# A gated recurrence on TensorE: 448-column f16 matmuls between its dependent matmuls, and its bias rows as two-row f16 matmuls

## The chip, the core and the metric

One core of one Trainium2 chip runs the whole program in one launch. The metric is the device time of one execution in microseconds (us). TensorE (PE; its weight loads are PEld) does the matmuls and writes PSUM, VectorE (DVE) and ScalarE (ACT) read PSUM and do the elementwise work, GpSimd (POOL) does memsets, copies and indirect DMAs, SyncE (SP) issues most transfers. Each has its own instruction stream; they meet at semaphores.

## What is computed

Four layers are applied to x of shape 8 x 512 x 256. Only the first has the part that is changed, a GRU over 512 time steps:

```python
def step(h, inp):                       # h: 8 x 256, one x_t of 8 x 256 a step
    x_t, prop = inp
    comb = jnp.concatenate([x_t, h], axis=-1)
    z = jax.nn.sigmoid(comb @ Wz + bz)
    r = jax.nn.sigmoid(comb @ Wr + br)
    comb2 = jnp.concatenate([x_t, r * h], axis=-1)
    h_cand = jnp.tanh(comb2 @ Wh + bh)
    h_new = (1.0 - z) * h + z * h_cand
    h_next = jnp.where(prop, jnp.tanh(h_new @ Wp + bp), h_new)
    return (h_next, h_new)
```

`prop` is true on every fourth step. What follows (a mixture-of-experts layer, a second one, a linear state-space layer with an LSTM-like layer, and a top-k layer) is not touched.

## The kernel before

Everything of the recurrence is held transposed: feature on the partition, batch of 8 on the free axis, two halves (k, m) of 128 features. The f32 hidden state is scaled by 256 and split into two f16 parts, `hpart[:, 0]` (high) and `hpart[:, 1]` (the rest); the recurrent weights are split likewise in `wpart`. A product with a gate is then 8 matmuls on part 0 and, once part 1 is there, 4 more (`recur`, L1418), each with 128x128 f16 weights of its own and 8 moving columns.

512 steps are made in 32 turns of 16. Each turn has four PSUM banks: r, z, candidate (c), and p, the bank of the propagated state. Of the p bank columns 0 to 63 are used. While one turn is stepped through, the input's share and the biases of the next turn are put into the other four banks by a generator, `projections`: for each of r, z, c and each half m, one f32 bias matmul with one row (`gbias` times `ones`, L1398) and two f32 matmuls of 128 columns with the input (`wx` times XT, L1402); then two f32 bias matmuls of 32 columns for p (L1406). These 20 items of a turn are taken one by one: one behind each step's c product, and one behind each of the four p products. PE's order within a step is: r (24 instructions with z), then c, then an item, and on every fourth step p, then an item. An f32 matmul shows as two instructions in the trace.

ACT reads the r, z, c (and p) banks with a tanh each; DVE makes `rhpart` from r and h (L905, L906, L908) and `hpart` from z, the candidate and h (L919 to L924). PE's loop runs over pairs of turns, so it branches back 15 times.

Ahead of the recurrence x is transposed on PE and copied by DVE to XT, ACT and DVE split the weights (L880), and DVE scales the biases (L883), which the first projections wait for.

Of the kernel before, what the change touches and what calls it, by code (L numbers as in the profile page):

```python
# [19 lines left out]
ALU = mybir.AluOpType  # L20
# [14 lines left out]
GSCALE = HSCALE * WSCALE  # L35
E = 8
# [22 lines left out]
def build_program(nc, t, out):  # L59
    ctx = ExitStack()  # L60
    with ctx:
        def sb(name, shape, dt=F32):
            return ctx.enter_context(nc.sbuf_tensor(name, shape, dt))
# [23 lines left out]
        gbias = sb("gbias", [1, 4, D])  # L87
# [17 lines left out]
        zeros = WA[:, 0:ZW]  # L105
        strict = sb("strict", [P, P])
# [114 lines left out]
        gru_b_loaded = sem("gru_b_loaded")  # L221
        wsplit, wsplit_high = sem("wsplit"), sem("wsplit_high")
        condT_psum = sem("condT_psum")
        condT_ready = sem("condT_ready")
# [5 lines left out]
        keep_ready, keep_h_ready, upd_ready = sem("keep_ready"), sem("keep_h_ready"), sem("upd_ready")  # L230
# [91 lines left out]
        def _(sp):  # L322
# [13 lines left out]
            for g, n in enumerate(("br", "bz", "bh", "bp")):  # L336
                sp.dma_start(gbias[0:1, g], t["L0_cond_" + n].rearrange("(a m) -> a m", a=1)).then_inc(gru_b_loaded, 16)
# [38 lines left out]
            sp.wait_ge(prefer_ready, E + 8)  # L376
# [84 lines left out]
            sp.wait_ge(prefer_ready, E + 9)  # L461
# [24 lines left out]
        def _(pool):  # L486
            nc.gpsimd.memset(ident[:], 0.0).then_inc(ident_zero, 1)
# [6 lines left out]
            nc.gpsimd.memset(ones16[:], 1.0).then_inc(prefer_ready, 1)  # L494
            nc.gpsimd.memset(strict[:], 1.0).then_inc(prefer_ready, 1)
            nc.gpsimd.memset(zeros, 0.0).then_inc(prefer_ready, 1)
            pool.wait_ge(prefer_ready, E + 6)
# [371 lines left out]
        def _(dve):  # L869
            for k in range(KD):  # L870
# [11 lines left out]
            dve.wait_ge(gru_b_loaded, 5 * 16)  # L882
            nc.vector.tensor_scalar(gbias[:], gbias[:], GSCALE, None, ALU.mult).then_inc(wsplit, 1)  # L883

            dve.wait_ge(condT_psum, 1)
            nc.vector.tensor_copy(condT[:].rearrange("p k b -> p (k b)"), banks[6][:, 0:KD * B]).then_inc(condT_ready, 1)
# [12 lines left out]
            with dve.Fori(0, TURNS) as it:  # L899
                for s in range(STEPS):  # L900
                    n = it * STEPS + s
                    h = entry_s[:] if s % CHUNK == 0 else hist[:, s - 1]

                    dve.wait_ge(r_ready, n + 1)
                    nc.vector.scalar_tensor_tensor(rhpart[:, 0], gate_r[:], 1.0, h, ALU.add, ALU.mult).then_inc(rh_part, 1)  # L905
                    nc.vector.scalar_tensor_tensor(rfull[:], gate_r[:], 1.0, h, ALU.add, ALU.mult).then_inc(rh_full, 1)  # L906
                    dve.wait_ge(rh_full, n + 1)
                    nc.vector.tensor_tensor(rhpart[:, 1], rfull[:], rhpart[:, 0], ALU.subtract).then_inc(rh_part, 1)  # L908

                    dve.wait_ge(z_ready, n + 1)  # L910
                    nc.vector.tensor_scalar(keep[:], gate_z[:], -0.5, 0.5, ALU.mult, ALU.add).then_inc(keep_ready, 1)
                    dve.wait_ge(keep_ready, n + 1)
                    nc.vector.tensor_tensor(keep_h[:], keep[:], h, ALU.mult).then_inc(keep_h_ready, 1)
                    if s % (STEPS // 2) == 0:

                        dve.wait_ge(hist_copied, it * 2 + 1 + s // (STEPS // 2))

                    dve.wait_ge(c_ready, n + 1)
                    nc.vector.scalar_tensor_tensor(upd[:], gate_z[:], 1.0, cand[:], ALU.add, ALU.mult).then_inc(upd_ready, 1)  # L919
                    dve.wait_ge(upd_ready, n + 1)  # L920
                    nc.vector.scalar_tensor_tensor(hpart[:, 0], upd[:], 0.5 * HSCALE, keep_h[:], ALU.mult, ALU.add).then_inc(h_part, 1)  # L921
                    nc.vector.scalar_tensor_tensor(hist[:, s], upd[:], 0.5 * HSCALE, keep_h[:], ALU.mult, ALU.add).then_inc(h_full, 1)  # L922
                    dve.wait_ge(h_full, n + 1)
                    nc.vector.tensor_tensor(hpart[:, 1], hist[:, s], hpart[:, 0], ALU.subtract).then_inc(h_part, 1)  # L924
                    if (s + 1) % CHUNK == 0:
                        split_entry(it * NP + (s // CHUNK + 2))

            link = Link(dve, vc)
# [61 lines left out]
            dve.wait_ge(prefer_ready, E + 8)  # L990
# [377 lines left out]
        def _(pe):  # L1368

            pe.wait_ge(const_ready, 2)  # L1370
# [8 lines left out]
            pe.wait_ge(gru_b_loaded, 5 * 16)  # L1379
# [6 lines left out]
            pe.wait_ge(gru_b_loaded, 5 * 16)  # L1386
# [6 lines left out]
            def projections(it, r_bank, z_bank, c_bank, p_bank):  # L1393

                for g, bank in enumerate((r_bank, z_bank, c_bank)):
                    for m in range(KD):
                        o = bank[:, m * W:(m + 1) * W]
                        nc.tensor.matmul(o, gbias[0:1, g, m * P:(m + 1) * P], ones[0:1, 0:W], start=m == 0, stop=False,  # L1398
                                         skip_group_check=True)
                        yield  # L1400
                        for k in range(KD):
                            nc.tensor.matmul(o, wx[:, g, k, m * P:(m + 1) * P], xview[:, k, bass.ds(it * STEPS, STEPS)],  # L1402
                                             start=False, stop=False, skip_group_check=True)
                            yield
                for m in range(KD):
                    nc.tensor.matmul(p_bank[:, m * NP * B:(m + 1) * NP * B], gbias[0:1, 3, m * P:(m + 1) * P],  # L1406
                                     ones[0:1, 0:NP * B], start=m == 0, stop=False, skip_group_check=True)
                    yield
# [479 lines left out]
```

## Time and profile before

| | us |
|---|---|
| median of 3 runs | 3479.25 (3477.07 to 3480.55) |
| span of the profiled execution, first to last instruction | 3475.2 |
| median less span, what lies around it | 4.05 |
| transposes, splits and first projections | 0 to 42.6 |
| recurrence | 42.6 to 1411 |
| everything after it | 1411 to 3475.2 |

The profiled execution has no time of its own listed beside its span, so the median of the runs stands for it. PE is busy for 2975.7 us (86%), DVE for 1343.1 (39%), ACT for 850.8 (24%), POOL for 431.1 (12%). Busy time of PE is from the start of a matmul to its modelled end, so overlapping matmuls fill it even where the engine moves few columns. The granted TensorE clock has two levels in this trace, 0.5 (1.2 GHz) and 1.0 (2.4 GHz).

### The profile page before, as it was taken

Reading aid. Unit: us, or ns where it says so; the run is one execution under the profiler, and the core shown is the slowest. Engines: PE = TensorE matmul, PEld = TensorE weight load, DVE = VectorE, ACT = ScalarE, POOL = GpSimd, SP = SyncE. Lnnn points to the kernel's source line nnn. Section 1 sums busy time; section 2 is a strip of 40 time slices with the busy share of each in tenths; the row PEclk is TensorE's granted clock in tenths of the full one; section 3 lists DMA queues with packets and bytes.
Section 4 is the critical chain, followed back from the end, with each engine's and each line's share of the span. In section 5 each row is a group of like instructions: output and inputs, shape, how many; then the busy total and the mean of one; then the engine's idle time right before and its main releaser. Section 6 shows DMA issues by size and latency. Waiting matters only on the chain.

```text
span 3475.2 us, 75119 instructions
## 1 busy us (share of the span) xinstructions
PE 2975.7 (86%) x28154; PEld 2213.9 (64%) x28154; DVE 1343.1 (39%) x6282; ACT 850.8 (24%) x2694; POOL 431.1 (12%) x510
## 2 busy tenths in 40 slices
PE   7888888888888888529999995789965898999888
PEld 6777777777777777318888883345841343388367
DVE  4555555555555555301111002433333356511442
ACT  1222222222222222112223221123521112322332
POOL 0000000000000000240000003343143000000343
PEclk6555555555555555659999997989987999899989
DMA  5000000000000000036666663312434431000123
GB/s 189 2 2 2 2 2 2 2 2 2 2 2 2 2 2 2 32 126 191 190 190 191 193 197 93 95 60 91 127 100 138 91 73 24 0 0 0 35 80 106
DMA packets 182176, 230.13 MB, mean 66 GB/s; under 512 B 57492, under 2 KB 146168, under 8 KB 181432
## 3 DMA queue, kind: packets, MB, share of 16 engines
q1 hardware_dynamic: 159704, 162.01, 16.4%
q0 software_dynamic: 22240, 64.51, 5.6%
q8 instruction: 209, 3.42, 0.4%
q14 instruction: 23, 0.19, 0.0%
HBM read 166.31 MB, written 60.16 MB: 65 GB/s over the span
## 4 chain that ended last, share of the span: by engine, by line
issue 46%; PE 44%; DVE 3%; DMA 2%; another core or an unknown queue 1%; POOL 1%; ACT 1%; SPq 1%; ACTq 0%; DVEq 0%; POOLq 0%
PE bank L1556 8%; PE bank L1568 8%; PE bank L1754 5%; PE bank L1513 3%; PE bank L1502 3%; PE bank L1614 2%; PE bank L1682 2%; PE bank L1671 2%; PE bank L1855 2%; PE bank L1867 2%; PE bank L1623 1%; PE bank L1716 1%; PE bank L1543 1%; PE bank L1789 1%
## 5 line engine op out<-in xcount | busy, mean ns | idle before, releaser
L1418 PEld LDWEIGHTS bank<-hpart,WB 128*128 128x128 f16 x13824 | 464.5, 105 | 229.4 <-DVE hpart L921 162.8
L1418 PE MATMUL bank<-hpart,WB 128*128 128x8 f16 x13824 | 520.4, 170 | 71.2 <-issue 45.3
L1418 PE MATMUL bank<-rhpart,WB 128*128 128x8 f16 x6144 | 288.1, 171 | 85.3 <-DVE rhpart L905 85.3
L1418 PEld LDWEIGHTS bank<-rhpart,WB 128*128 128x128 f16 x6144 | 242.3, 106 | 131.1 <-DVE rhpart L905 128.6
L1556 PE MATMUL bank<-WA,WB 128*128 128x256 f32 x1248 | 309.2, 381 | 8.7 <-DMA WA<-in_L_ffn_b 8.7
L1568 PE MATMUL bank<-WB,hid 128*128 128x256 f32 x1248 | 313.8, 379 | 0.0
L1402 PE MATMUL bank<-XT,WB 128*128 (+1 forms) x792 | 305.1, 482 | 0.9
L1556 PEld LDWEIGHTS bank<-WA,WB 128*128 128x128 f32 x1248 | 238.1, 191 | 41.7 <-issue 9.1
L1568 PEld LDWEIGHTS bank<-WB,hid 128*128 128x128 f32 x1248 | 234.2, 190 | 30.3
L1013 DVE COPY WA<-bank 128x512 f32<-128x512 f32 x76 | 52.6, 692 | 514.6 <-PE bank L1543 514.6
L671 ACT ACTIVATE hid<-bank,b_up 128x256 f32<-128x256 f32 x312 | 148.0, 475 | 394.2 <-PE bank L1556 394.2
L596 ACT ACTIVATE gate_r<-bank 128x16 f32<-128x16 f32 x512 | 94.7, 185 | 598.0 <-PE bank L1418 598.0
L1402 PEld LDWEIGHTS bank<-XT,WB 128*128 128x128 f32 x792 | 198.6, 312 | 4.8 <-issue 1.3
L510 POOL TENSOR_TENSOR HT<-hist,unscale 128x128 f32 x64 | 29.5, 460 | 1374.2 <-DVE hist L922 1374.2
L600 ACT ACTIVATE cand<-bank 128x16 f32<-128x16 f32 x512 | 94.2, 184 | 279.2 <-PE bank L1418 279.2
L1398 PE MATMUL bank<-ones,gbias 1*128 1x128 f32 x396 | 156.5, 496 | 3.8 <-DVE gbias L883 3.8
L905 DVE SCALAR_TENSOR_TENSOR rhpart<-gate_r,hist 128x16 f16<-128x16 f32 x384 | 67.5, 176 | 223.0 <-ACT gate_r L596 223.0
L919 DVE SCALAR_TENSOR_TENSOR upd<-gate_z,cand 128x16 f32<-128x16 f32 x512 | 90.0, 176 | 149.7 <-ACT cand L600 149.7
L523 POOL DMA_INDIRECT tile_rows<-WA,slots x128 | 123.4, 964 | 158.3 <-ACT WA L708 77.2
L528 POOL DMA_DIRECT2D expert_rows<-WA x78 | 56.0, 718 | 696.5 <-DVE WA L1024 530.0
L543 POOL DMA_INDIRECT WA<-expert_rows,slots x128 | 121.7, 951 | 90.5 <-DVE WA L1035 46.8
L1614 PE MATMUL bank<-XT,WB 128*128 (+1 forms) x256 | 118.3, 611 | 7.7 <-DVE WB L1076 7.6
(305 smaller groups left out, 4010.6 us busy)
## 6 DMA issues: line engine op xcount, KB each, us to landing
WB<-in_L_ffn_w SPq DMA_DIRECT2D x78, 1024.0 KB, 7.8
WA<-tile_rows SPq DMA_DIRECT2D x86, 256.0 KB
expert_rows<-WA POOLq DMA_DIRECT2D x86, 256.0 KB, 2.7
GB<-gates SPq DMA_DIRECT2D x8, 2048.0 KB
tile_rows<-WA SPq DMA_DIRECT2D x4, 2496.0 KB, 17.6
WA<-in_L_ffn_b SPq DMA_DIRECT2D x40, 128.0 KB, 7.3
GB<-in_x SPq DMA_DIRECT2D x8, 512.0 KB, 7.1
out<-HT SPq DMA_DIRECT2D x16, 256.0 KB
```

What stands on the lines that cost most here:

```text
L523: nc.gpsimd.indirect_dma_start(xg, bass.IndirectOffsetOnAxis(ap=slots[:, c, b:b + 1], axis=0), hrow[:, q], None).then_inc(moved[q], 16)
L543: nc.gpsimd.indirect_dma_start(grow[:, q, c], None, yg, bass.IndirectOffsetOnAxis(ap=slots[:, c, b:b + 1], axis=0)).then_inc(moved[q], 16)
L671: nc.scalar.activation(hid0[:, f], banks[f % RING][:, 0:ET], ACT.Gelu, bias=b0_up[:, i, f:f + 1]).then_inc(S["hid_ready"], 1)
L1398: nc.tensor.matmul(o, gbias[0:1, g, m * P:(m + 1) * P], ones[0:1, 0:W], start=m == 0, stop=False, skip_group_check=True)
L1402: nc.tensor.matmul(o, wx[:, g, k, m * P:(m + 1) * P], xview[:, k, bass.ds(it * STEPS, STEPS)], start=False, stop=False, skip_group_check=True)
L1418: last = nc.tensor.matmul(bank[:, m * width + s * B:m * width + (s + 1) * B], wpart[:, g, w, k, m * P:(m + 1) * P], part[:, a, k * B:(k + ...
L1502: last = nc.tensor.matmul(banks[f % RING][:], up(f, k), src(k), start=k == 0, stop=k == KD - 1)
L1513: last = nc.tensor.matmul(banks[4 + m][:], down(h, m), hid[:, h % RING], start=h == 0 and not out_extra, stop=h == n - 1)
L1556: last = nc.tensor.matmul(banks[f % RING][:, 0:ET], w0_up[i][:, k, f * P:(f + 1) * P], xgT[:, i, k], start=k == 0, stop=k == KD - 1)
L1568: last = nc.tensor.matmul(banks[4 + m][:, 0:D], hid0[:, h, half_of(m)], w0_down[i][:, h], start=h == 0, stop=h == F0 - 1)
L1614: last = nc.tensor.matmul(banks[u % RING][:], (wsh1, wsh3)[u % 2][:, k, u // 2 * P:(u // 2 + 1) * P], XT[:, k, cols(j)], start=k == 0, sto ...
L1754: last = nc.tensor.matmul(banks[h * 3 + g][:, m * 256:(m + 1) * 256], uT[:, g + 4 * part, k, half_of(m)], src, start=not part and m == 0 a ...
```

## The change

Two things are done in the recurrence, and the start is rearranged for them.

1. `keep_clock` issues f16 matmuls of 448 columns with operands that are always there (`wpart`) into columns 64 to 511 of the next turn's p bank, which nothing reads. One stands between z and c in each step, two behind the item after c, one behind the item after p, and one more at either place where the item was a bias.
2. A bias item becomes one f16 matmul with two rows: the high and the low f16 part of the bias (`gbias_part`) times 256 (`bias_unit`). It has no f32 matmul any more.
3. Ahead of the first projections 24 matmuls of 512 columns on ones are issued (`BURST`). The bias loads are issued first of all DMAs, with a semaphore of their own for `condrow`; DVE splits the biases ahead of its copies of x; POOL makes the constants for it first. Two unused semaphores go.

```diff
+BURST = 24
+STREAM = 2
...
+            for g, n in enumerate(("br", "bz", "bh", "bp")):
+                sp.dma_start(gbias[:, g], t["L0_cond_" + n].rearrange("(a m) -> a m", a=1).partition_broadcast(2)).then_inc(gru_b_loaded, 16)
             for j in range(B // 2):
                 load_x(j)
-            sp.dma_start(condrow[:], t["cond_1024"]).then_inc(gru_b_loaded, 16)
+            sp.dma_start(condrow[:], t["cond_1024"]).then_inc(condrow_loaded, 16)
...
+            dve.wait_ge(gru_b_loaded, 4 * 16)
+            dve.wait_ge(row_made, 4)
+            link(nc.vector.tensor_scalar(gbias, gbias, HSCALE, None, ALU.mult))
+            link(nc.vector.tensor_copy(gbias_hi, gbias))
+            link(nc.vector.tensor_tensor(gbias_rest, gbias, gbias_hi, ALU.subtract))
+            link(nc.vector.tensor_scalar(gbias_rest, gbias_rest, part_row[:, 1:2], None, ALU.mult))
+            nc.vector.scalar_tensor_tensor(gbias_part, gbias_hi, part_row[:, 0:1], gbias_rest, ALU.mult, ALU.add
+                                           ).then_inc(wsplit, 1)
...
+            ones512 = ones16[:].rearrange("p (a c) -> p a c", a=1).to_broadcast([P, 512 // P, P])
+            for i in range(BURST):
+                nc.tensor.matmul(banks[7][:], ones16[:], ones512, start=i == 0, stop=i == BURST - 1)
             pe.wait_ge(gru_w_loaded, 7 * 16)
...
-                        nc.tensor.matmul(o, gbias[0:1, g, m * P:(m + 1) * P], ones[0:1, 0:W], start=m == 0, stop=False,
+                        nc.tensor.matmul(o, gbias_part[:, g, m * P:(m + 1) * P], bias_unit[:, 0:W], start=m == 0, stop=False,
                                          skip_group_check=True)
-                        yield
+                        yield True
...
+            spare = slice(KD * NP * B, 512)
+            stream = wpart[:, 3, 0].rearrange("p k m -> p (k m)")[:, spare]
+
+            def keep_clock(bank, count):
+
+                for _ in range(count):
+                    nc.tensor.matmul(bank[:, spare], wpart[:, 3, 0, 0, 0:P], stream, start=False, stop=True, skip_group_check=True)
...
                     recur(gates[1], 1, W, s, hpart, None).then_inc(z_psum, 1)
+                    keep_clock(next_gates[3], 1)
                     recur(gates[2], 2, W, s, rhpart, lambda a: pe.wait_ge(rh_part, n * 2 + a + 1)).then_inc(c_psum, 1)
-                    next(following, None)
+                    light = next(following, True)
+                    keep_clock(next_gates[3], STREAM + light)
                     if (s + 1) % CHUNK == 0:
                         recur(gates[3], 3, NP * B, s // CHUNK, hpart,
                               lambda a: pe.wait_ge(h_part, n * 2 + a + 1)).then_inc(p_psum, 1)
-                        next(following, None)
+                        light = next(following, True)
+                        keep_clock(next_gates[3], 1 + light)
```

PE's order in a step of the loop, before. L1418 are the products, L1402 an input item, L1398 a bias item; ISA and REGISTER_ALU are waits and counting:

```order
L1402 ISA
L1402 MATMUL bank<-XT,WB 128x128
L1418 MATMUL bank<-hpart,WB 128x8 x24
L1435 ISA
L1418 MATMUL bank<-rhpart,WB 128x8 x8
L1435 REGISTER_ALU
L1418 MATMUL bank<-rhpart,WB 128x8 x4
L1398 MATMUL bank<-ones,gbias 128x128
L1418 MATMUL bank<-hpart,WB 128x8 x12
L1402 MATMUL bank<-XT,WB 128x128
```

PE's order at the same place of the changed kernel. L1440 are the products, L1452 the new 448-column matmuls, L1424 an input item, L1420 a bias item:

```order
L1424 ISA
L1424 MATMUL bank<-XT,WB 128x128
L1452 MATMUL bank<-WB 128x448 x2
L1440 MATMUL bank<-hpart,WB 128x8 x24
L1452 MATMUL bank<-WB 128x448
L1466 ISA
L1440 MATMUL bank<-rhpart,WB 128x8 x8
L1466 REGISTER_ALU
L1440 MATMUL bank<-rhpart,WB 128x8 x4
L1420 MATMUL bank<-WA 128x128
L1452 MATMUL bank<-WB 128x448 x3
L1440 MATMUL bank<-hpart,WB 128x8 x12
```

The new matmuls stand between z's product and c's, and between the items and the next product on `hpart`; no product has changed its place among the others. A turn has 60 of them: 16 behind z, 32 and 6 behind the items after c, 4 and 2 behind the items after p.

PE's order ahead of the recurrence, before and then changed (transposes, then the first projections):

```order
L1377 MATMUL bank<-ident,GB 128x128 x64
L1381 MATMUL bank<-ident,condrow 128x8 x2
L1398 MATMUL bank<-ones,gbias 128x128
L1402 MATMUL bank<-XT,WB 128x128 x2
L1398 MATMUL bank<-ones,gbias 128x128
```

```order
L1397 MATMUL bank<-ident,GB 128x128 x64
L1401 MATMUL bank<-ident,condrow 128x8 x2
L1407 MATMUL bank<-ones 128x512 x24
L1420 MATMUL bank<-WA 128x128
L1424 MATMUL bank<-XT,WB 128x128 x2
```

The 24 burst matmuls stand where PE waited for the scaled biases.

## Rows read from the trace of the kernel before

**Rows 1.** Busy time by stretch, the recurrence: length, engines (instructions), granted clock, DMA.

```profile
42.60:1411.00 1368.40, 1211.00 (x21249) 1000.00 (x21248) 724.43 (x4991) 306.72 (x1664) 29.46 (x64) 0.50 0.02 6
```

**Rows 2.** Timeline of one step: start, length, engine, line, operation [idle before].

```profile
802.98 0.89 PE L1418 MATMUL bank<-hpart,WB 128*128 128x8 f16 x24
803.05 0.17 DVE L924 TENSOR_TENSOR hpart<-hist,hpart 128x16 f16<-128x16 f32 x1
803.59 0.18 ACT L596 ACTIVATE gate_r<-bank 128x16 f32<-128x16 f32 x1 [1.08 <-PE bank L1418]
...
804.04 0.57 PE L1418 MATMUL bank<-rhpart,WB 128*128 128x8 f16 x12 [0.17 <-DVE rhpart L905]
804.10 0.17 DVE L908 TENSOR_TENSOR rhpart<-rfull,rhpart 128x16 f16<-128x16 f32 x1
...
804.46 0.77 PE L1402 MATMUL bank<-XT,WB 128*128 x2
...
805.30 0.86 PE L1418 MATMUL bank<-hpart,WB 128*128 128x8 f16 x23
```

**Rows 3.** Timeline of PE: p products and what follows, then two loop starts.

```profile
189.29 0.56 PE L1418 MATMUL bank<-hpart,WB 128*128 128x8 f16 x12
...
190.51 0.80 PE L1418 MATMUL bank<-hpart,WB 128*128 128x8 f16 x24
...
199.73 0.56 PE L1418 MATMUL bank<-hpart,WB 128*128 128x8 f16 x12
...
200.78 0.87 PE L1418 MATMUL bank<-hpart,WB 128*128 128x8 f16 x24
...
214.38 0.80 PE L1418 MATMUL bank<-hpart,WB 128*128 128x8 f16 x24 [3.24 <-issue]
...
814.25 0.80 PE L1418 MATMUL bank<-hpart,WB 128*128 128x8 f16 x24 [3.21 <-issue]
```

**Rows 4.** Timeline of PE, the same f16 and f32 matmuls at either clock.

```profile
3288.10 0.24 PE L1831 MATMUL bank<-ones,GB 128*128 128x1 f16 x4
3288.22 0.24 PE L1831 MATMUL bank<-ones,GB 128*128 128x1 f16 x4
...
3302.84 0.24 PE L1831 MATMUL bank<-ones,GB 128*128 128x1 f16 x4
3302.98 0.24 PE L1831 MATMUL bank<-ones,GB 128*128 128x1 f16 x4
...
1411.02 6.40 PE L1467 MATMUL bank<-HT,rw 128*8 128x512 f32 x8
1417.69 1.88 PE L1467 MATMUL bank<-HT,rw 128*8 128x512 f32 x4
```

**Rows 5.** Busy time by stretch, columns as in rows 1, where the clock rose, stayed, fell.

```profile
31.00:41.00 10.00, 10.00 (x33) 7.71 (x33) 0.11 (x1) 0.00 (x0) 0.00 (x0) 0.50 1.05 443
1417.00:1430.00 13.00, 13.00 (x49) 3.58 (x48) 0.00 (x0) 4.07 (x6) 0.00 (x0) 1.00 0.00 0
3007.00:3027.00 20.00, 20.00 (x25) 7.36 (x24) 11.97 (x15) 8.81 (x15) 0.00 (x0) 0.51 0.00 1
...
3287.30:3289.00 1.70, 1.17 (x22) 0.93 (x23) 1.60 (x7) 0.71 (x2) 0.00 (x0) 1.00 0.00 0
3297.60:3300.30 2.70, 0.00 (x0) 0.00 (x0) 2.56 (x12) 0.59 (x2) 1.75 (x3) 1.00 0.14 49
3301.00:3304.00 3.00, 3.00 (x30) 2.66 (x30) 2.81 (x9) 1.45 (x4) 2.20 (x3) 0.50 0.54 173
```

**Rows 6.** Groups by line: PE's matmuls from 3007 to 3027.

```profile
L1727 PE MATMUL bank<-GB,WB 64*128 64x512 f32 x24 | 20.2, 1037 | 2.7 <-ACT HT L804 2.7
```

**Rows 7.** Timeline of the start: weight split, first projection, first step.

```profile
27.37 2.49 DVE L880 SCALAR_TENSOR_TENSOR WB<-WB 128x512 f16<-128x512 f32 x4
...
30.59 0.50 PE L1398 MATMUL bank<-ones,gbias 1*128 1x128 f32 x2 [3.83 <-DVE gbias L883]
...
42.58 0.80 PE L1418 MATMUL bank<-hpart,WB 128*128 128x8 f16 x24
```

More of the change, by code:

```diff
@@ L86, in build_program @@
         wpart = WB[:, 4096:6144].bitcast(F16).rearrange("p (g n k m) -> p g n k m", g=4, n=2, k=KD)
-        gbias = sb("gbias", [1, 4, D])
+        part_row = sb("part_row", [2, 2])
         hid = sb("hid", [P, RING, TILE])
@@ L105, in build_program @@
         zeros = WA[:, 0:ZW]
+        gbias, gbias_rest = (WA[0:2, ZW + i * 1024:ZW + (i + 1) * 1024].rearrange("p (g m) -> p g m", g=4) for i in range(2))
+        gbias_hi, gbias_part = (WA[0:2, ZW + 2048 + i * 512:ZW + 2560 + i * 512].bitcast(F16).rearrange("p (g m) -> p g m", g=4)
+                                for i in range(2))
+        bias_unit = WA[0:2, ZW + 3072:ZW + 3072 + STEPS * B // 2].bitcast(F16)
         strict = sb("strict", [P, P])
@@ L221, in build_program @@
         gru_b_loaded = sem("gru_b_loaded")
+        condrow_loaded = sem("condrow_loaded")
+        row_made = sem("row_made")
         wsplit, wsplit_high = sem("wsplit"), sem("wsplit_high")
         condT_psum = sem("condT_psum")
-        condT_ready = sem("condT_ready")
         r_psum, z_psum, c_psum, p_psum = (sem(f"{n}_psum") for n in "rzcp")
@@ L229, in build_program @@
         e_part, e_full = sem("e_part"), sem("e_full")
-        keep_ready, keep_h_ready, upd_ready = sem("keep_ready"), sem("keep_h_ready"), sem("upd_ready")
+        keep_ready, upd_ready = sem("keep_ready"), sem("upd_ready")
         hist_copied = sem("hist_copied")
@@ L373, in _ @@
             column(wr3[:], halves("L3_ffn_w_router")).then_inc(w3_loaded, 16)
-            sp.wait_ge(prefer_ready, E + 8)
+            sp.wait_ge(prefer_ready, E + 7)
             zrows = xg.rearrange("(p n) d -> p (n d)", p=P)
@@ L486, in _ @@
         def _(pool):
+            nc.gpsimd.memset(part_row[:, 0:1], 0.0).then_inc(row_made, 1)
+            nc.gpsimd.memset(part_row[:, 1:2], 1.0).then_inc(row_made, 1)
+            nc.gpsimd.memset(bias_unit, WSCALE).then_inc(const_ready, 1)
+            nc.gpsimd.memset(ones16[:], 1.0).then_inc(const_ready, 1)
+            pool.wait_ge(row_made, 2)
+            nc.gpsimd.memset(part_row[0:1, 0:1], 1.0).then_inc(row_made, 1)
+            nc.gpsimd.memset(part_row[0:1, 1:2], 0.0).then_inc(row_made, 1)
             nc.gpsimd.memset(ident[:], 0.0).then_inc(ident_zero, 1)
@@ L912, in _ @@
                     dve.wait_ge(keep_ready, n + 1)
-                    nc.vector.tensor_tensor(keep_h[:], keep[:], h, ALU.mult).then_inc(keep_h_ready, 1)
+                    nc.vector.tensor_tensor(keep_h[:], keep[:], h, ALU.mult)
                     if s % (STEPS // 2) == 0:
@@ L926, in _ @@
                         split_entry(it * NP + (s // CHUNK + 2))
-            link = Link(dve, vc)
             V = nc.vector
@@ L986, in place_tokens @@
                 V.tensor_copy(etab[:], one(2)).then_inc(etab_ready, 1)
-            dve.wait_ge(prefer_ready, E + 8)
+            dve.wait_ge(prefer_ready, E + 7)
             take_logits(0, r_log, E)
@@ L1368, in _ @@
         def _(pe):
-            pe.wait_ge(const_ready, 2)
+            pe.wait_ge(const_ready, 4)
             for j in range(B):
@@ L1378, in _ @@
                     last.then_inc(xT_psum[k], 1)
-            pe.wait_ge(gru_b_loaded, 5 * 16)
+            pe.wait_ge(condrow_loaded, 16)
             for k in range(KD):
@@ L1403, in projections @@
                                              start=False, stop=False, skip_group_check=True)
-                            yield
+                            yield False
                 for m in range(KD):
-                    nc.tensor.matmul(p_bank[:, m * NP * B:(m + 1) * NP * B], gbias[0:1, 3, m * P:(m + 1) * P],
-                                     ones[0:1, 0:NP * B], start=m == 0, stop=False, skip_group_check=True)
-                    yield
+                    nc.tensor.matmul(p_bank[:, m * NP * B:(m + 1) * NP * B], gbias_part[:, 3, m * P:(m + 1) * P],
+                                     bias_unit[:, 0:NP * B], start=m == 0, stop=False, skip_group_check=True)
+                    yield True
             def recur(bank, g, width, s, part, wait):
```

13 lines of the change are left out of this document (4 added, 9 removed).

## The prediction

> **What bounds the kernel now.** I read the busy time by stretch first: the recurrence takes 1368.4 us of the span, PE counts as busy for 1211.0 of them, and the granted clock is 0.50 throughout [rows 1]. The share of 88% does not make PE the bound. The timeline of one step shows why [rows 2]: r's product starts at 802.98 and the next step's at 805.30, 2.31 us later in nearly every step, and between them stand chains of PE, ACT and DVE. r starts, its tanh starts 0.61 us later, c's product starts 0.45 us behind that, the input item is issued at 804.46 behind c, and PE's next product waits for `hpart`. The second part of r's product waits for DVE's L924 (803.05 to 803.22), c's for L908 (804.10 to 804.27), whatever PE's speed. The last c matmul is issued at about 804.44, so PE has 0.86 us there for the item, which needs about 0.6; between z's last matmul (issued 0.17 before 803.87, about 803.70) and c it has 0.33 us. An f32 item is thus free today.
>
> Every fourth step has p as well: from p's start to the next r it is 1.05 us with an input item behind p (199.73 to 200.78) and 1.22 us with a bias item (189.29 to 190.51) [rows 3]. That happens once a turn with a full bias item. Two loop starts, seven pairs of turns apart, stand at 214.38 and 814.25: 85.70 us a pair; less the 3.24 us that PE stands idle at the branch, a turn is 41.2 us.
>
> **What a faster clock could give.** The small matmuls hardly depend on it. Five f16 matmuls (four of L1831 and one of the line behind) take from 3288.10 to 3288.22 at the full clock, some 25 ns each, and from 3302.84 to 3302.98 at half, some 27 [rows 4, 5]; the recurrence's 24 in 0.89 us, less the last one's latency of 0.17 and a wait of 0.06, fit 27 [rows 2]. I write 26.7. On the chain of a step lie two tails of four such matmuls and two latencies. Counting 2 ns a matmul and a few ns a latency and weight load, a step gains 0.02 to 0.04 us; I take 0.03. Over 512 steps that is 15 us, over 128 p products another 2. The bias item behind p falls from two f32 instructions to one short f16 one: 0.17 us x 32 turns = 5.4 us, at either clock if nothing takes its place. The large f32 matmuls do halve (8 in 6.40 us, then 4 in 1.88 [rows 4]), but these are hidden. So a perfectly held full clock is worth about 23 us of 1368.
>
> **What the 448-column matmuls cost.** No row shows an f16 matmul of this width. From below: one column in each clock cycle of the granted level gives 373 ns at 1.2 GHz and 187 ns at 2.4. From above: an f32 instruction of 512 columns starts each 0.8 us at half clock [rows 4], which for 448 columns is 700 ns, but an f32 product is made in two such instructions, and its operands are twice as wide. I take the lower end, since the f16 8-column rows show no such surcharge; with the upper end at half clock each turn would grow by a further 60 x 0.33 = 20 us, which I don't believe. The Trainium skill ("TensorE: Matmul & The Clock Gate", back-to-back issue gap) would have 373 and 189 ns; by it the sum below stays as it is.
>
> At the full clock all of it fits: 0.19 in the 0.33 us ahead of c; an input item (about 0.3) and two (0.38), or a bias (0.06) and three (0.57), in the 0.86 us behind c; and behind p, 0.49 in about 0.65. The cost is nothing, and the cover is the DVE and ACT chain.
>
> At half clock it does not fit. PE becomes the chain: r and z 24 x 26.7 ns = 0.64 us; 0.37; c's second part can't start before DVE's L908, at 1.24, and ends at 1.37 with its wait; an input item 0.59 and 0.75 behind it. That makes 2.72 us instead of 2.31; a step with a bias item 1.37 + 0.11 + 1.12 = 2.60. `hpart` is then ready before PE is. Of a turn's twelve steps without p, eight have an input item and four a bias: 8 x 2.72 + 4 x 2.60 = 32.2 us. A step with p is 1.37 + item and stream + 0.34 + item and stream: 3.92, 3.92, 4.03 and 3.65 us for the four pairs of items, together 15.5. A turn is 47.7 us instead of 41.2, and 32 turns cost 208 us.
>
> **Which clock it will have.** This decides. Rows 5 and 6 are read for what PE did before the clock rose or fell. It rose after 1411, when wide f32 matmuls over all 128 partitions ran with no gap (the 8 of rows 4, and 1.00 from 1417 to 1430). It stayed at 0.50 from 31 to 41, though PE is busy for all 10.00 us: there f32 items of 128 columns alternate with one-row bias matmuls. It stayed at 0.51 from 3007 to 3027, also all busy, where the matmuls are 512 columns wide but on 64 partitions [rows 6]. So a busy row is not enough: narrow, one-row and half-height matmuls did not bring the clock up. And it fell behind a stretch of 2.70 us without a matmul (3297.6 to 3300.3), to 0.50 from 3301.
>
> In the changed loop the wide matmuls are full height, which speaks for a rise. Against it: of a half-clock step's 2.72 us the 36 eight-column matmuls hold PE for about 0.96 with next to nothing moving, and each pair of turns has the 3.2 us at the branch [rows 3], longer than the gap that brought the fall above. Even if the burst starts the recurrence at full clock, that gap comes 15 times, and a full-clock step has PE standing still for about a fifth of it. After a fall PE must earn the rise in steps that are again a mixture like those that stayed at half. I think it more likely than not that it doesn't.
>
> **The start.** Today PE waits for the weight split and the scaled bias (L880 from 27.37, first projection at 30.59), then projects until 42.58 [rows 7]. Four bias DMAs ahead of x and the memsets ahead of `ident` move the transposes by about 1 us; DVE's five bias operations lie ahead of its first copy. The burst takes 24 x 0.21 = 5 us from about 28.5 if the clock is full, 10 us if half; the projections then take 4 us instead of 12 at full clock. I take 4 us off; the ends are 6 off and 5 on. The tail after 1411 only shifts.
>
> **The sum.** 3475.2 + 208 - 4 = 3679, and 4.05 around it gives 3683; the median is that of the runs, with which the span and its surroundings agree by construction. I put 3684.
>
> **Rivals.**
> - Full clock held: chance 0.29. Wide full-height matmuls fill nearly every hole of the step. 23 us and 4 us come off: 3452. It ends faster. It decides from the point where about nine tenths of the recurrence run at full clock, since each tenth at half costs 23 us against full. The Trainium skill ("TensorE: Matmul & The Clock Gate", why this matters) says that TensorE gets its full clock when it is kept busy and has no long idle gaps; by that rule PE, which has no hole at all in the half-clock loop, would be lifted soon after every branch, and the result would be this one. The stretches of rows 5 at 0.50 with PE busy throughout do not agree.
> - The clock goes up and down, some turns at full: 0.09. Full against half is 208 + 23 = 231 us; with half of the time at either level 208 - 116 = 92 us on, about 3570.
> - The wide matmuls leave the clock at half but do so at little cost, or nine tenths are full, so that it cancels: 0.03, 3479.
> - Half clock with a change-over from f32 to f16 weights on the chain as well: behind a bias item it is 1.22 against 1.05 us [rows 3], so up to 0.12 us more for each of the 12 input items: 46 us on, 3730. It is the upper end of the likeliest case, which holds 0.59 in all, 3655 to 3735.
>
> **How the numbers follow.** Likeliest is half clock, 3684. The full-clock case is too likely to be left out, so the range reaches from 3440 (its gain doubled on the chain) to 3735; beyond it I leave the f32 price of the wide matmuls and a start that loses more. Less than 0.2% (7 us) can't be told from no change by runs that spread over 3.5 us. Faster 0.30, same 0.03, slower 0.67.
>
> **What would show it.** In the changed trace: granted clock of the recurrence near 0.50; r's start to r's start 2.72 or 2.60 us, with no idle time of PE ahead of r; the 448-column matmul at about 373 ns apart; `cand`'s wait for PE unchanged and `gate_r`'s longer; first r at 38 to 40 us. Wrong, if the clock is 0.9 or more there and steps are 2.28 us; then the stretches that I compare with were no likeness of this loop. Wrong in size, if wide f16 matmuls cost more than a column a cycle.

## The result: 3728.7 us, and the profile after

| | us |
|---|---|
| kernel before, median beside it | 3478.16 (3474.21 to 3480.55) |
| changed kernel, median | 3728.7 (3727.36 to 3729.85) |
| ratio, 95% interval | 1.0721 (1.0708 to 1.0733) |
| span of its profiled execution | 3725.6 |

The changed kernel is 250 us slower. The forecast was 3684, with 3655 to 3735 for its likeliest case; the measured time lies 44.7 us above the forecast and inside both ranges. In the experiments a median takes in every execution, while a ratio leaves out those over 1.5% above the fastest of their kernel (one of 4456 us in run 1, one each in runs 6 and 9).

From the page of the changed kernel: the granted clock in 40 equal slices of the span, and the group of the new matmuls (busy us, mean ns of one).

```profile
PEclk6555555555555555555899999799997799889989
...
L1452 PE MATMUL bank<-WB 128*128 128x448 f16 x1920 | 915.9, 560 | 0.0
```

Busy time by stretch of the changed kernel, columns as in [rows 1]: the burst and the first projections, the first step, the recurrence.

```profile
28.00:39.00 11.00, 10.77 (x47) 6.03 (x48) 3.08 (x10) 0.00 (x0) 0.00 (x0) 1.00 0.86 316
39.20:44.00 4.80, 4.80 (x54) 3.16 (x53) 1.31 (x9) 0.55 (x3) 0.00 (x0) 0.50 1.07 458
...
44.00:1660.00 1616.00, 1581.11 (x22863) 1082.50 (x22862) 722.78 (x4980) 305.87 (x1660) 29.56 (x64) 0.50 0.02 5
```

The burst did bring the clock up, for most of the projections. It fell at 39 us, two microseconds before the first step began, while PE was busy with projections: from 28 to 39 it had stood idle for 0.23 us, and from 39.2 to 44 not at all. So here the clock fell without a hole in PE's work. It did not come back for 1616 us, although PE counts as busy for 97.8% of them. [Rows 1] show 0.50 with 88%. So the recurrence grew from 1368 to more than 1616 us with no change in its clock.

Timeline of PE, changed kernel: a step with a bias item, the step behind it, one with an input item, and one with p.

```profile
800.29 0.83 PE L1440 MATMUL bank<-hpart,WB 128*128 128x8 f16 x24
...
801.30 0.54 PE L1440 MATMUL bank<-rhpart,WB 128*128 128x8 f16 x12
801.77 0.28 PE L1420 MATMUL bank<-WA 2*128 2x128 f16 x1
801.99 1.30 PE L1452 MATMUL bank<-WB 128*128 128x448 f16 x3
803.08 0.83 PE L1440 MATMUL bank<-hpart,WB 128*128 128x8 f16 x24
...
805.99 0.83 PE L1440 MATMUL bank<-hpart,WB 128*128 128x8 f16 x24
...
807.01 0.54 PE L1440 MATMUL bank<-rhpart,WB 128*128 128x8 f16 x12
807.41 0.77 PE L1424 MATMUL bank<-XT,WB 128*128 x2
808.00 0.93 PE L1452 MATMUL bank<-WB 128*128 128x448 f16 x2
808.72 0.83 PE L1440 MATMUL bank<-hpart,WB 128*128 128x8 f16 x24
...
812.82 0.83 PE L1440 MATMUL bank<-hpart,WB 128*128 128x8 f16 x24
```

No row has a bracket: PE waits for nothing that the trace shows, where in [rows 2] it stood idle ahead of c. PE has become the chain. The wide matmuls start 0.36 us apart (three of them, then r: 801.99 to 803.08; two: 808.00 to 808.72); one column a cycle at 1.2 GHz would be 0.37. A step with an input item is 2.73 us (805.99 to 808.72), one with a bias item 2.79 (800.29 to 803.08), one with p 4.10 (808.72 to 812.82). ACT shows the same from its side: summed over the recurrence, its idle time ahead of `gate_r` grew from 598 to 770 us, and that ahead of `cand` stayed at 279, as the prediction's signs had it.

Two loop starts of the changed kernel, seven pairs of turns apart:

```profile
142.72 0.80 PE L1440 MATMUL bank<-hpart,WB 128*128 128x8 f16 x24 [2.46 <-issue]
...
852.32 0.80 PE L1440 MATMUL bank<-hpart,WB 128*128 128x8 f16 x24 [2.36 <-issue]
```

That is 101.37 us a pair, and less 2.41 us of idle time 49.5 us a turn, against 41.2 before [rows 3].

### The profile page after: what moved, and what is told of

Its sections match the earlier page's. It is cut to its first block, busy times and chain, and to the rows that moved or that the text cites. A ratio compares the mean times of both kernels' runs of the same rounds, so it can differ in the third digit from the quotient of the medians.

```text
span 3725.6 us, 78489 instructions
## 1 busy us (share of the span) xinstructions
PE 3357.3 (90%) x29834; PEld 2301.1 (62%) x29834; DVE 1350.3 (36%) x6286; ACT 851.3 (23%) x2694; POOL 432.3 (12%) x515
## 4 chain that ended last, share of the span: by engine, by line
issue 50%; PE 42%; DVE 3%; DMA 1%; another core or an unknown queue 1%; POOL 1%; SPq 1%; ACT 1%; DVEq 0%; ACTq 0%; POOLq 0%
PE bank L1589 7%; PE bank L1601 7%; PE bank L1787 5%; PE bank L1546 3%; PE bank L1535 3%; PE bank L1647 3%; PE bank L1715 2%; PE bank L1704 2%; PE bank L1888 2%; PE bank L1900 1%; PE bank L1656 1%; PE bank L1576 1%; PE bank L1822 1%; PE bank L1749 1%
## 5 line engine op out<-in xcount | busy, mean ns | idle before, releaser
L1452 PE MATMUL bank<-WB 128*128 128x448 f16 x1920 | 915.9, 560 | 0.0
L1440 PEld LDWEIGHTS bank<-hpart,WB 128*128 128x128 f16 x13824 | 521.0, 108 | 317.2 <-issue 183.9
L1440 PE MATMUL bank<-hpart,WB 128*128 128x8 f16 x13824 | 488.4, 170 | 34.0 <-issue 34.0
L1440 PEld LDWEIGHTS bank<-rhpart,WB 128*128 128x128 f16 x6144 | 245.9, 109 | 114.6 <-DVE rhpart L926 114.6
L1424 PE MATMUL bank<-XT,WB 128*128 (+1 forms) x792 | 304.6, 481 | 0.9
L1440 PE MATMUL bank<-rhpart,WB 128*128 128x8 f16 x6144 | 279.1, 173 | 0.0
L1452 PEld LDWEIGHTS bank<-WB 128*128 128x128 f16 x1920 | 207.3, 120 | 95.0 <-issue 42.8
L1424 PEld LDWEIGHTS bank<-XT,WB 128*128 128x128 f32 x792 | 197.7, 309 | 4.1
```

The lines of the kernel that those rows point to most:

```text
L1440: last = nc.tensor.matmul(bank[:, m * width + s * B:m * width + (s + 1) * B], wpart[:, g, w, k, m * P:(m + 1) * P], part[:, a, k * B:(k + ...
L1452: nc.tensor.matmul(bank[:, spare], wpart[:, 3, 0, 0, 0:P], stream, start=False, stop=True, skip_group_check=True)
```

## The experiments

Three questions: do the wide matmuls at half clock make the whole cost; what makes the bias item dearer than forecast; and can more wide work hold the clock, and would that pay? All runs are timed against the kernel before. Line numbers of the experiments' rows shift by one to three. Runs 5, 9 and 10 were timed on another chip than the other experiments, each with the kernel before on the same chip, so kernels are compared by their ratios.

**1. Bias rows and start as changed, no 448-column matmul.**

```diff
-                    keep_clock(next_gates[3], 1)
-                    keep_clock(next_gates[3], STREAM + light)
-                        keep_clock(next_gates[3], 1 + light)
```

> The changed kernel without any of the 448-column matmuls; the bias items and the start are as changed. Theory A (the wide matmuls, at half clock, make PE the chain): the whole loss goes. The recurrence is at 0.50, steps 2.31 us, no 0.17 us behind the one bias item a turn (5 us less), and whatever the start gives: 3470, from 3462 to 3480. Rival B (the two-row bias items carry a good part of the loss, by about 0.2 us each, even without the wide matmuls): 8 x 32 x 0.2 = 51 us stay, near 3520.

Measured: 3470.8, ratio 0.9989 (0.9976 to 1.0002). PE in this run:

```profile
803.01 0.56 PE L1440 MATMUL bank<-rhpart,WB 128*128 128x8 f16 x12 [0.17 <-DVE rhpart L926]
...
805.32 0.56 PE L1440 MATMUL bank<-rhpart,WB 128*128 128x8 f16 x12 [0.17 <-DVE rhpart L926]
```

A holds. The steps are those of the kernel before, c to c 2.31 us (803.01 to 805.32), and PE waits 0.17 us for `rhpart` again. So the 250 us need the wide matmuls. The p step gives back what was forecast: from p to the next r it is 1.05 us with a bias item behind p (785.96 to 787.01), where it had been 1.22. But at the loop start at 810.85 PE stands idle for 3.57 us instead of 3.24. The bias rows by themselves bring at most a quarter of a per cent, and no gain is shown: the interval reaches 1.0002.

**2. Only the one between z and c.**

```diff
                     keep_clock(next_gates[3], 1)
-                    keep_clock(next_gates[3], STREAM + light)
-                        keep_clock(next_gates[3], 1 + light)
```

> The changed kernel with the wide matmuls between z and c alone (16 a turn); those behind the items are out. Theory A: c's second part waits for DVE anyway, so this one is free even at half clock, and the time is that of the kernel without any, to 3 us. Rival C (each wide matmul costs its 0.33 to 0.37 us wherever it stands, or slows ACT and DVE by contention): 512 x 0.36 = 184 us more than without, or a good part of it.

Measured: 3473.75, ratio 1.0003 (0.9991 to 1.0016), as run 1 (A, not C). At half clock the hole ahead of c takes one wide matmul for nothing: 0.33 us of room, 0.33 us used. The cost comes in with the two or three behind the items.

**3. The wide matmuls 128 columns wide.**

```diff
+            spare = slice(KD * NP * B, KD * NP * B + P)
+            stream = stream[:, 0:P]
```

> The changed kernel with its wide matmuls 128 columns wide instead of 448, the same number at the same places. Theory H (column time at the half clock is all that the wide matmuls cost): 128 columns take 107 ns at 1.2 GHz. In a step with an input item they and the item take 0.59 + 0.21 us in the 0.86 us behind c, with a bias item 0.31 + 0.32 us, and 0.11 of the 0.33 us ahead of c; steps return to about 2.31 us and the time to that of the kernel without them, 3470 (3465 to 3482); the granted clock stays at 0.50. Theory I (each such matmul costs something that doesn't go by its columns, as a change-over or its weight load): they still delay each step by two to three times 0.05 us or more, at 16 steps x 32 turns at least 50 us, 3520 or above. Results are those of the reference, since the wide matmuls write to unused columns.

Measured: 3472.8, ratio 1.0001 (0.9989 to 1.0013). H holds. The number of matmuls, their places and their weight loads are those of the changed kernel, and the 250 us are gone. The timeline of PE:

```profile
800.78 0.88 PE L1440 MATMUL bank<-hpart,WB 128*128 128x8 f16 x24
...
802.84 0.40 PE L1455 MATMUL bank<-WB 128*128 128x128 f16 x2
803.09 0.89 PE L1440 MATMUL bank<-hpart,WB 128*128 128x8 f16 x24
```

Item and two narrow ones fit behind c, and the step is 2.31 us again (800.78 to 803.09). Column time is what the changed loop pays for, and only where it overflows its hole.

**4. The bias operands 128 rows high.** The rows 2 to 127 are zero, so the sum is the same and each bias matmul is a 128x128 one.

```diff
-        bias_unit = WA[0:2, ZW + 3072:ZW + 3072 + STEPS * B // 2].bitcast(F16)
+        gbias_part = WA[:, 8192 - 512:8192].bitcast(F16).rearrange("p (g m) -> p g m", g=4)
+        bias_unit = WA[:, 8192 - 576:8192 - 512].bitcast(F16)
...
+            nc.gpsimd.memset(gbias_part, 0.0).then_inc(row_made, 1)
```

> The changed kernel with the bias operands made 128 rows high (the further rows of the weights are zero); wide matmuls as changed. Theory F (the bias item cost 0.3 us instead of the 0.11 us of my sum, because the change between two rows and 128 rows of the array keeps the weight loads from running ahead): a bias item falls by some 0.2 us, 8 a turn, 32 turns: 45 to 50 us less than the changed kernel, near 3680. Rival G (the excess is of another kind, such as the time of any f16 matmul of 128 columns behind the register work): no change to 5 us, 3725.

Measured: 3647.2, ratio 1.0495 (1.0470 to 1.0521), some 80 us less than the changed kernel. PE, at half clock:

```profile
802.47 0.83 PE L1441 MATMUL bank<-hpart,WB 128*128 128x8 f16 x24
...
803.49 0.54 PE L1441 MATMUL bank<-rhpart,WB 128*128 128x8 f16 x12
803.88 0.27 PE L1421 MATMUL bank<-WA 128*128 128x128 f16 x1
803.95 1.33 PE L1453 MATMUL bank<-WB 128*128 128x448 f16 x3
805.07 0.83 PE L1441 MATMUL bank<-hpart,WB 128*128 128x8 f16 x24
```

From c's start to the first wide matmul it is now 0.46 us (803.49 to 803.95); with two-row operands it was 0.69 (801.30 to 801.99). The step is 2.60 us (802.47 to 805.07), which is the forecast's number. So F holds: the height of the bias operands costs 0.2 us an item, about 50 of the 80 us. The rest goes with the clock: this run shows 0.56 over the recurrence. That puts 12% of the 1530 us, 184 us or some 80 steps, at 1.00, where a step with an input item takes 2.28 us (352.00 to 354.28) instead of 2.73; an estimate of 36 us from these figures.

```profile
45.00:1575.00 1530.00, 1486.72 (x22670) 1022.86 (x22669) 716.66 (x4938) 303.51 (x1645) 29.08 (x63) 0.56 0.02 5
```

**5. Each bias matmul of r, z and c twice in a row.** These biases count twice in the output.

```diff
+                        nc.tensor.matmul(o, gbias_part[:, g, m * P:(m + 1) * P], bias_unit[:, 0:W], start=False, stop=False,
+                                         skip_group_check=True)
```

> The changed kernel with each of a turn's six bias matmuls of r, z and c issued twice in a row (the biases of the gates count twice, so the output is another). Bias item steps there took 0.2 us more than forecast. Theory T (the price is a change-over between operands two rows high and 128 rows high, paid once on each side of the item): the second one adds its columns alone, 0.11 us x 6 x 32 = 21 us, 3750. Theory U (each two-row matmul has the price by itself): 0.31 us x 192 = 60 us, 3788.

Measured: 3748.3, ratio 1.0777 (1.0762 to 1.0793), 19.6 us above the changed kernel, where T gave 21 and U 60.

```profile
810.16 0.54 PE L1442 MATMUL bank<-rhpart,WB 128*128 128x8 f16 x12
810.63 0.28 PE L1420 MATMUL bank<-WA 2*128 2x128 f16 x1
810.72 0.31 PE L1422 MATMUL bank<-WA 2*128 2x128 f16 x1
810.96 1.30 PE L1454 MATMUL bank<-WB 128*128 128x448 f16 x3
```

The second one starts 0.09 us behind the first, and the wide ones 0.24 behind it, as behind the single one (0.22). The price is thus not one of the two-row matmul but of the change from 128 rows to two and back: 0.08 us ahead (c to item 0.47 us, against 0.39 in run 4), and 0.15 behind (0.22, against 0.07).

**6. More of them: two between z and c, one more everywhere else.**

```diff
-STREAM = 2
+STREAM = 3
...
-                    keep_clock(next_gates[3], 1)
+                    keep_clock(next_gates[3], 2)
...
-                        keep_clock(next_gates[3], 1 + light)
+                        keep_clock(next_gates[3], 2 + light)
```

> The changed kernel with more wide matmuls: two between z and c, three (four behind a bias) behind the items after c, two (three) behind the items after p; 120 a turn less 20, that is 100 instead of 60. Theory A with D (the clock was missed by little, and more wide full-height matmuls in a step bring it up and keep it but for some us behind each branch): the granted clock of the recurrence is 0.9 or more, steps are 2.3 to 2.4 us, the time 3470 to 3520. Rival E (the eight-column matmuls and the branch keep this loop at half clock whatever is added): each turn grows by 40 x 0.36 less what lies in waits, some 12 us, 400 us in all, near 4130.

Measured: 3697.1 (3682.8 to 3747.9), ratio 1.0623 (1.0595 to 1.0650). The profiled execution has a span of 3746.2 us, so it is read for its steps and not for its sum. By the edit a turn has 96 wide matmuls (32 between z and c, 54 behind the items after c, 10 behind those after p), not the 100 of the expectation. By stretch:

```profile
44.00:100.00 56.00, 56.00 (x688) 35.33 (x687) 20.48 (x141) 8.60 (x47) 0.46 (x1) 0.50 0.23 95
108.00:145.00 37.00, 37.00 (x653) 27.11 (x652) 19.39 (x135) 8.24 (x45) 0.46 (x1) 1.00 0.01 3
```

Neither forecast holds. With 96 wide matmuls a turn the kernel is faster than with 60, since the clock did rise; but it also fell again and again, and is 0.77 over the recurrence of this execution. At 1.00 a step with an input item is 2.42 us (188.56 to 190.98), at 0.50 it is 3.44 (611.44 to 614.88).

**7. Two between z and c, all else as changed.**

```diff
-                    keep_clock(next_gates[3], 1)
+                    keep_clock(next_gates[3], 2)
```

> The changed kernel with two wide matmuls instead of one between z's and c's product. Theory J (more wide work at this place brings the clock up for part of the recurrence, as it did in the run with more wide matmuls everywhere, where it was 0.77): the granted clock of the recurrence lies between 0.6 and 0.9, with stretches at 1.00 that end at no particular place; steps at 1.00 take 2.3 to 2.4 us, steps at 0.50 take 0.33 us more than in the changed kernel, 3.0 to 3.1; at half of the time at each level 3590 to 3700. Theory K (it stays at half): each of 512 steps is 0.33 us longer, 3729 + 169 = 3898, less where p's steps hide some. Theory L (held at full): 3470.

Measured: 3866.1 (3841.5 to 3878.4), ratio 1.1144 (1.1110 to 1.1179). The clock was 0.54 over the recurrence of the profiled execution, the shortest of four, and the step behind a branch took 3.10 us (801.95 to 805.05). That is nearly K, the case in which it stays at half, for 3898.

**8. Both: bias operands 128 rows high, and two between z and c.** The edits are those of runs 4 and 7.

> The changed kernel with both edits: the bias operands 128 rows high (zeros in rows 2 to 127, the product is the same) and two wide matmuls between z's and c's product. Theory J: full-height work in every step is the largest so far for its length, so the granted clock of the recurrence is above that of either edit alone, 0.8 or more, with steps of 2.3 to 2.4 us at 1.00; 3480 to 3560. Theory M (the clock goes up and down at some rate of its own whatever is added): clock as in the run with two alone, and a time 30 to 50 us below it from the cheaper bias items.

Measured: 3494.3 (3475.0 to 3514.1), ratio 1.0067 (1.0044 to 1.0090). By stretch: behind one branch of the loop, from there to the next branch, and the recurrence up to 1395.

```profile
208.80:212.00 3.20, 3.20 (x44) 1.88 (x43) 1.66 (x13) 0.65 (x4) 0.00 (x0) 0.50 0.00 0
212.20:293.80 81.60, 77.42 (x1409) 54.86 (x1407) 43.32 (x298) 18.16 (x99) 1.84 (x4) 1.00 0.01 2
...
45.00:1395.00 1350.00, 1287.32 (x22731) 901.76 (x22728) 703.84 (x4847) 296.12 (x1616) 28.59 (x62) 0.94 0.02 6
```

This is nearly the rival "full clock held". The clock stays up for a whole pair of turns and falls behind the branch, where PE stands still. The timeline of PE shows two such loop starts, a step at 0.50 in one of the longer stretches down (551 to 569), and one at 1.00:

```profile
122.69 0.76 PE L1441 MATMUL bank<-hpart,WB 128*128 128x8 f16 x24 [2.92 <-issue]
...
207.92 0.76 PE L1441 MATMUL bank<-hpart,WB 128*128 128x8 f16 x24 [2.93 <-issue]
...
555.58 0.83 PE L1441 MATMUL bank<-hpart,WB 128*128 128x8 f16 x24
...
558.64 0.83 PE L1441 MATMUL bank<-hpart,WB 128*128 128x8 f16 x24
...
803.58 0.80 PE L1441 MATMUL bank<-hpart,WB 128*128 128x8 f16 x24
...
804.62 0.50 PE L1441 MATMUL bank<-rhpart,WB 128*128 128x8 f16 x12
804.97 0.67 PE L1425 MATMUL bank<-XT,WB 128*128 x2
805.46 0.56 PE L1453 MATMUL bank<-WB 128*128 128x448 f16 x2
805.86 0.80 PE L1441 MATMUL bank<-hpart,WB 128*128 128x8 f16 x24
```

A step is 2.28 us (803.58 to 805.86) instead of 2.31, as forecast for the full clock. At 0.50 it is 3.06 (555.58 to 558.64), since there two wide ones ahead of c don't fit. A pair of turns with one short fall is 85.23 us (122.69 to 207.92) instead of 85.70. Sixteen times 0.47 us would be 8 us gained. But a clock of 0.94 means that 12% of the 1350 us, 162 us, ran at 0.50, and at 3.06 us a step instead of 2.28 they cost about 162 x 0.78 / 3.06 = 41 us. Of J's "0.8 or more, 3480 to 3560" both parts hold, and the kernel is 0.4 to 0.9% slower than before.

**9 and 10. As run 8, with fewer wide matmuls behind bias items, and more right behind the branch.** Run 9 has a third one behind c only in the first step behind the branch, run 10 in the first three; neither has it behind bias items elsewhere.

```diff
-                    keep_clock(next_gates[3], STREAM + light)
+                    keep_clock(next_gates[3], STREAM + (looped and s < 1))
```

```diff
-                    keep_clock(next_gates[3], STREAM + light)
+                    keep_clock(next_gates[3], STREAM + 1 if looped and s < 3 else STREAM)
```

> Bias operands 128 rows high, two wide matmuls between z's and c's product, always two behind c; a third only in the first step behind the loop's branch, and none extra behind a bias item elsewhere. In the run with the third behind every bias item, steps at 1.00 took 2.28 us with an input item and 2.35 with a bias item and three wide matmuls, steps with p 3.31, and the clock fell behind every branch. Theory P (at 1.00 the third wide matmul is what makes a bias step longer than 2.28): six or so bias steps a turn lose 0.07 us x 32 turns, 10 to 13 us less than that run, 3481, if the clock stays up elsewhere. Theory Q (the clock then also falls at other places than behind the branch, since these steps hold less wide work): clock of the recurrence under 0.9, time above 3500.

> As the kernel with the third wide matmul in the first step behind the branch only, but in the first three steps behind it. Theory R (more wide work right behind the branch brings the clock back sooner): each stretch at 0.50 is a short one, none of some 20 us as in the run before at 550 and 638; the clock of the recurrence is 0.95 or more and the time 3460 to 3475, so level with the kernel before or up to 0.4% faster. Theory S (how long it stays down is not a matter of these steps): the same stretches as with one, and a time within 5 us of it.

Measured: 3536.0, ratio 1.0132 (1.0096 to 1.0168), and 3547.0, ratio 1.0217 (1.0192 to 1.0242). Run 9, the recurrence by stretch, and on PE, at 1.00, c of a step with a bias item and the next r:

```profile
45.00:1480.00 1435.00, 1348.76 (x23139) 935.69 (x23138) 720.06 (x4971) 303.53 (x1656) 29.36 (x64) 0.85 0.02 6
```

```profile
766.28 0.50 PE L1441 MATMUL bank<-rhpart,WB 128*128 128x8 f16 x12
...
766.69 0.54 PE L1453 MATMUL bank<-WB 128*128 128x448 f16 x2
767.48 0.85 PE L1441 MATMUL bank<-hpart,WB 128*128 128x8 f16 x24 [0.24 <-DVE hpart L943]
```

P and R fell, Q holds, and S's "within 5 us" was missed (11 us). With two wide matmuls PE waits 0.24 us for DVE, and c to r is 1.20 us anyway: the third one had been free, and without it PE has a hole in six steps a turn. The clock came down to 0.85 in both runs, and more wide matmuls right behind the branch did not help: run 10 has the higher ratio, though single executions of run 9 lie between 3498 and 3582 us. Run 8 was not timed on the chip of these two, so a part of the chip in the lower clock is not ruled out.

**11. A burst of one matmul instead of 24.**

```diff
-BURST = 24
+BURST = 1
```

> The changed kernel with 1 matmul of 512 columns ahead of the projections instead of 24. Theory N (the burst buys a full clock for the projections and costs its own 5.3 us): without it the projections start 5 us earlier and run at half clock, 12 us instead of 7.6; the first r comes within 1 us of 41.1, the recurrence is at 0.50 as before and the time is 3729 within 5. Theory O (the burst also decides at which clock the recurrence begins and so more than its own time): the time differs by more than 10 us either way.

Measured: 3720.8 (3714.2 to 3724.7), ratio 1.0718 (1.0694 to 1.0742), no different in ratio from the changed kernel's; O's difference of more than 10 us is not there. First projection and first r:

```profile
29.80 0.26 PE L1420 MATMUL bank<-WA 2*128 2x128 f16 x1 [2.03 <-DVE WB L903]
...
38.18 0.80 PE L1440 MATMUL bank<-hpart,WB 128*128 128x8 f16 x24
```

At half clock the projections take 8.4 us (29.80 to 38.18). In the changed kernel the burst runs at 1.00, and so do they up to 39:

```profile
28.23 5.34 PE L1407 MATMUL bank<-ones 128*128 128x512 f16 x24 [0.77 <-DVE XT L898]
33.51 0.23 PE L1420 MATMUL bank<-WA 2*128 2x128 f16 x1
...
41.11 0.80 PE L1440 MATMUL bank<-hpart,WB 128*128 128x8 f16 x24
```

That is 7.6 us (33.51 to 41.11), for a burst of 5.3. The burst loses 2.9 us, more than "within 1 us" said.

No version measured here beats the kernel before beyond doubt; the nearest is run 1, 0.1% below it with an interval that reaches over 1.

## Why the prediction came out as it did

**The clock, the step that decides: right.** I put it at half with 0.59, because [rows 5] show PE busy throughout at 0.50 where much of what it does is narrow or not full height, and because the loop's branch leaves PE idle. The recurrence ran at 0.50 for 1616 us. The Trainium skill ("TensorE: Matmul & The Clock Gate", why this matters) would have had it lifted; the trace does not agree.

What I had not seen is how near it was, and in that the right answer was in part luck. Runs 4, 6 and 8 lift it to 0.56, 0.77 and 0.94. My argument "a mixture like those that stayed at half" holds for this mixture only. The number of wide matmuls alone does not order the runs: with two-row bias operands 60, 76 and 96 a turn gave 0.50, 0.54 and 0.77, with operands 128 rows high 60 and 76 gave 0.56 and 0.94. Nor was the branch what kept the clock down here: it was down before the first step, and in run 8, which has the same branch, it came back.

**The worth of a full clock: right in the step, and small.** The step of 2.28 us was forecast and run 8 shows it. The forecast for a clock that never falls was 27 us below the kernel before, 23 of them in the recurrence and 4 at the start. Run 8's 3494.3 less the 41 us that its stretches at 0.50 cost is 3453, which is 20 us below the 3473.5 of the kernel before beside it; 5 of these 20 are the start, since the first r comes at 37.35 there and not at 42.58 [rows 7]. That leaves about 15 us for the recurrence. This is an estimate, since no run held the clock throughout. In one thing the forecast erred: at 1.00 the input item does not take 0.3 us but 0.49 (804.97 to 805.46), against 0.59 at 0.50 (807.41 to 808.00). With two wide ones it is 0.89 us (804.97 to 805.86), a little over the 0.86 of the hole, so that PE never waits there.

**The wide matmul's price: right.** About one column a cycle, 0.36 us at half clock and 0.20 at full (805.46 to 805.86 for two). Run 3 shows that nothing else about it costs as long as the holes take it.

**The bias item: the step of the sum that failed in size.** "A step with a bias item 1.37 + 0.11 + 1.12 = 2.60": it took 2.79. I had counted its 128 columns and not the change of height on both sides. (Ahead of c two small errors cancel: the 24 products of r and z took 0.68 us, 800.29 to 800.97, and not 0.64, the wide matmul behind them 0.33 and not 0.37.) In the steps with p, 3.92 became 4.10. Run 4 removed exactly this (2.60), and run 5 showed that it is paid for each change and not for each matmul. My own rival had a change-over in it, but at the f32 items, which cost none: 2.73 against 2.72.

The price stood in [rows 3], and I read it otherwise. The 1.22 us with a bias item behind p and the 1.05 with an input item differ in these two rows, each two f32 instructions of 128 columns, the one with one row and the other with 128:

```profile
189.79 0.79 PE L1398 MATMUL bank<-ones,gbias 1*128 1x128 f32 x2
...
200.16 0.77 PE L1402 MATMUL bank<-XT,WB 128*128 x2
```

From p to the item it is 0.50 us against 0.43, and from the item to the next r 0.72 against 0.62. I had taken these 0.17 us for the price of two f32 instructions, and in the rival for a change from f32 to f16. They are of the size of the price of height that runs 4 and 5 measured, though no run varied the height of the f32 item alone.

I had missed a rule there. The Trainium skill ("TensorEngine Tiling (Array Packing)", key properties) says that a change of the tiling mode, and not just of the tile, drains TensorE. Whether a two-row operand is such a change of mode, or another cause tied to height makes the 0.23 us of the two changes, no run here tells apart.

**The first input item of a turn** follows register instructions of PE, and its step is longer than 2.73. I put it down to them, which no run shows by itself:

```profile
804.09 0.54 PE L1440 MATMUL bank<-rhpart,WB 128*128 128x8 f16 x12
804.66 0.79 PE L1424 MATMUL bank<-XT,WB 128*128 x2
```

It is 2.91 us (803.08 to 805.99), 0.57 instead of 0.40 from c to the item. Before, that stood in a hole.

**The branch and the start.** The idle time at the branch shrank from 3.24 [rows 3] to 2.4 us, which the sum had left as it was. For the start I took 4 us off; the first r comes at 41.11 instead of 42.58 [rows 7], 1.5 us off. With the burst the projections were to take 4 us. They took 7.6, and 8.4 without it: most of the gain over the 12 us before is that of the f16 bias rows.

The terms against the forecast:

| term | forecast | measured | difference |
|---|---|---|---|
| turn, without the branch | 47.7 | 49.5 | 32 x 1.8 = +58 |
| branch | 3.24 | 2.41 | 15 x -0.83 = -12 |
| start | -4 | -1.5 | +2.5 |
| sum | | | +48 |

That meets the 44.7 us above the forecast within 4 us. Of the 1.8 us a turn the eight bias items make about 1.5 and the item behind the register instructions 0.2.

**What stays open:** the rise and fall of the clock in run 6, why it fell in the projections of the changed kernel, and why runs 9 and 10 came down to 0.85. Shown is that more wide matmuls together with high bias rows bring it up; what makes it fall where PE has no hole is not.

## What to carry to other kernels

Before paying for a faster clock, add up what on the chain would get faster: here the chain is made of 8-column matmuls and engine latencies, and the full clock gave 0.03 us of a 2.31 us step. Filler is free only while it fits the hole at the clock that the engine has now; if it brings the clock up only sometimes, it is paid at the dearer rate. Keep small helper matmuls at the height of their neighbours: the zero rows of run 4 cost nothing, a change of height cost 0.2 us wherever PE had no hole.

## What the hardware showed that I had not expected

- Two rows among 128: 0.08 us ahead and 0.15 behind the item at half clock (runs 4 and 5). At full clock the first projections show it too. In run 8, with bias rows 128 high, a group of one bias and four input matmuls takes 0.97 us (32.42 to 33.39) at 1.00; in the changed kernel, two rows high and also at 1.00, 1.21 (33.51 to 34.72).
- f32 matmuls of 128 columns do not halve at the full clock: four of them take 1.16 us at 0.50 (29.99 to 31.15 in run 11) and 0.90 at 1.00 (31.52 to 32.42 in run 8). Those of 512 columns do [rows 4].
- PE stayed at 1.2 GHz for 1616 us in which its only idle time was some 2.4 us at each branch of the loop, and the clock had fallen to that level with no idle time just ahead.
- In all seven kernels with the burst and two-row bias operands (the changed one, runs 1 to 3 and 5 to 7) the clock fell in the projections or within 2 us behind them, between 37 and 43 us, while PE was busy. In all four with bias operands 128 rows high (runs 4 and 8 to 10) it held through the projections, and past 45 us. Whether it is the height or the longer time that the two-row projections take is not shown.
- Two edits together did what neither did alone: the clock was 0.54 with two wide ones ahead of c, 0.56 with high bias rows, 0.94 with both.
